# Moving the gating and most of the expert choice of a mixture-of-experts layer into the tail of the attention before it

## What is computed

```python
scores = jax.nn.sigmoid(x @ gate_w)                       # x: layernormed rows, 2048 x 512
group_scores = jnp.max(scores.reshape(T, 4, 8), axis=-1)
_, top_groups = jax.lax.top_k(group_scores, 2)            # scores outside them: -inf
_, selected_experts = jax.lax.top_k(masked_scores, 6)
weights = take_along_axis(scores, selected_experts); weights = weights / sum(weights)
# rows sorted by expert, then for each expert
d = (silu(xs @ w_gate[e]) * (xs @ w_up[e])) @ w_down[e]
expert_out = sum over the six of d * weight
shared = silu(x @ sw_gate) * (x @ sw_up) @ sw_down
return expert_out + shared
```

## Time and profile before

| | us |
|---|---|
| median of 3 runs | 2407.72 (2406.47 to 2412.87) |
| profiled execution | 2406.69 |
| its span, first to last instruction | 2404.6 |
| TensorE busy | 1983.8 (83%) |
| VectorE busy | 1051.7 (44%) |
| GpSimd busy | 1149.9 (48%) |
| ACT busy | 542.0 (23%) |
| mean granted clock of TensorE | 0.911 |

### The profile page before, as it was taken

The page is one execution under the profiler, slowest core; times in us unless marked ns, Lnnn a source line. Parts: engine busy times, 40 slices in busy tenths (PEclk is TensorE's granted clock), DMA queues, the critical chain, the costliest instruction groups (busy, mean ns, idle before and its releaser), DMA issues. The chain is left out here.

```text
span 2404.6 us, 33128 instructions
## 1 busy us (share of the span) xinstructions
PE 1983.8 (83%) x10463; PEld 1425.6 (59%) x10464; DVE 1051.7 (44%) x2035; ACT 542.0 (23%) x1148; POOL 1149.9 (48%) x578
## 2 busy tenths in 40 slices
PE   6947887968854889998699969999999999999910
PEld 3414443423322334332499959999999999999810
DVE  2564442067673567673575323333333333333300
ACT  3221221101102445442212212222221222222100
POOL 0000000003552465553615667667666878781886
PEclk8977997979985889999799989999999999999965
DMA  3051004121114344451304445545545555553999
GB/s 111 0 150 57 18 27 174 45 80 53 70 70 153 116 153 159 151 174 58 111 25 181 161 144 164 167 156 162 159 163 163 175 163 184 172 163 90 207 156 195
DMA packets 199484, 305.23 MB, mean 127 GB/s; under 512 B 16472, under 2 KB 94808, under 8 KB 199416
## 3 DMA queue, kind: packets, MB, share of 16 engines
q1 hardware_dynamic: 141624, 186.98, 24.5%
q0 software_dynamic: 21504, 50.74, 9.3%
q10 hardware_dynamic: 36288, 66.59, 8.0%
HBM read 186.16 MB, written 118.10 MB: 127 GB/s over the span
## 5 line engine op out<-in xcount | busy, mean ns | idle before, releaser
L2091 PE MATMUL psum<-e_gu_high,e_rowT_high 128*128 (+1 forms) x1272 | 428.7, 338 | 1.8 <-issue 1.6
L2091 PE MATMUL psum<-e_gu_low,e_rowT_high 128*128 (+1 forms) x1272 | 411.0, 325 | 0.0
L1744 ACT ACTIVATE e_silu<-psum 128x352 f32<-128x352 f32 x159 | 74.0, 466 | 867.0 <-PE psum L2096 844.9
L2096 PE MATMUL psum<-e_gu_high,e_rowT_low 128*128 (+1 forms) x1272 | 257.3, 324 | 11.3 <-DVE e_rowT_low L1812 11.3
L2091 PEld LDWEIGHTS psum<-e_gu_high,e_rowT_high 128*128 128x128 f32 x1272 | 240.4, 189 | 24.1 <-issue 18.8
L2091 PEld LDWEIGHTS psum<-e_gu_low,e_rowT_high 128*128 128x128 f32 x1272 | 241.4, 190 | 4.1
L2096 PEld LDWEIGHTS psum<-e_gu_high,e_rowT_low 128*128 128x128 f32 x1272 | 214.5, 189 | 11.6 <-DVE e_rowT_low L1812 11.6
L1821 DVE TENSOR_TENSOR e_midT_low<-psum,e_midT_high 128x256 fp32r<-128x256 f32 x159 | 67.4, 424 | 312.8 <-ACT e_midT_high L1753 310.5
L2111 PE MATMUL psum<-e_d_high,e_midT_high 128*128 (+3 forms) x477 | 188.8, 396 | 1.0 <-ACT e_midT_high L1753 1.0
L1717 POOL DMA_INDIRECT X<-d_y,f_slots x96 | 148.1, 1543 | 83.9 <-DVE e_y L1841 53.3
L2111 PE MATMUL psum<-e_d_low,e_midT_high 128*128 (+3 forms) x477 | 188.0, 394 | 0.0
(11 more groups left out here) (338 smaller groups left out, 3669.7 us busy)
## 6 DMA issues: line engine op xcount, KB each, us to landing
d_sorted<-y_zeros SPq DMA_DIRECT2D x32, 1040.0 KB, 8.6
d_y<-e_y ACTq DMA_DIRECT2D x127, 256.0 KB
e_row<-d_sorted ACTq DMA_DIRECT2D x125, 260.0 KB
e_gu_in<-in_L_ffn_w_gate SPq DMA_DIRECT2D x32, 704.0 KB, 4.4
e_gu_in<-in_L_ffn_w_up SPq DMA_DIRECT2D x32, 704.0 KB, 5.0
e_d_in<-in_L_ffn_w_down SPq DMA_DIRECT2D x32, 512.0 KB
d_y<-y_zeros SPq DMA_DIRECT2D x8, 1024.0 KB, 5.6
e_d_in<-in_L_ffn_w_down SPq DMA_DIRECT2D x32, 192.0 KB
```

Of the source, the lines that this page charges most:

```text
L2091: nc.tensor.matmul(bank[:, 0:M].unsqueeze(1), rowT_high[par][:, k, :], w[:, bass.ds(buffer, 1), k, at:at + M], start=(k == 0 and n == 0), ...
L2096: last = nc.tensor.matmul(bank[:, 0:M].unsqueeze(1), rowT_low[par][:, k, :], gu_high[:, bass.ds(buffer, 1), k, at:at + M], start=False, st ...
```

## The change

- `hold_routing` keeps `hs`, set 0's input tiles, the gate weights, the small constants and an arena of SBUF through both stages; tiles of the attention are laid over them (for instance `prob` for even groups over the arena, the q and k rows over set 0's input), and so the waits on what lies below change.
- In the attention VectorE makes the spread of a batch (`row_spread`) in groups 9 and 13, GpSimd its power, VectorE the normed rows (`norm_row`) of batch 0 in groups 10 and 11 and of batch 1 in groups 14 and 15, each behind the group's last `find_max`. The zero stores are spread over 12 groups.
- The loop ends at group 15; what followed is written out by hand. TensorE turns and gates batches 0 and 1, then 2, between the sums and values of the last group; projects tiles 12 to 15 in two alternating banks; then turns and gates batch 3. The choice for tiles 0 to 11 (class `Choice`) runs on VectorE between the last `add_out`s, up to `mark_hot` and `add_members`.
- SP loads set 0 at the end of the attention. In the new stage the split of set 0 is shared: ACT and VectorE make the gate part's high and low, GpSimd the rest; then GpSimd splits set 1.
- VectorE makes the whole choice for tiles 12 to 15 ahead of `shared_steps(0)`, marks and counts before `shared_steps(1)`. `COUNTED` goes from 7 to 2, `PLACED` from 9 to 4, `find_slots(0)` comes after tile 3, the last after tile 5.
- A row carries all six weights and all six expert numbers (524 floats). The column copies and their waits are gone. A routed tile picks its weight with `scalar_tensor_tensor`: columns whose expert number equals the tile's expert, times weights, summed in the accumulator.

```diff
-            for g in range(GROUPS + 6):
-                if 1 <= g <= GROUPS:
+            for g in range(GROUPS):
+                if g >= 1:
                     invert_sums(g - 1)
...
+                if g in (9, 13):
+                    row_spread(g // 4 - 2)
+                if g in (10, 11, 14, 15):
+                    t = g // 4 * JT - 2 * JT + g % 2 * 2
+                    norm_row(t)
+                    norm_row(t + 1)
+            add_out(11)
+            row_spread(2)
+            invert_sums(GROUPS - 1)
+            for t in range(2 * JT, 3 * JT):
+                norm_row(t)
+            scale_values(GROUPS - 1, 0)
+            scale_values(GROUPS - 1, 1)
+            dve.wait_ge(choice_loaded, 5 * 16)
+            dve.wait_ge(exped, 1)
+            first.invert()
+            add_out(12)
+            first.rank_groups()
+            add_out(13)
+            first.find_top()
+            add_out(14)
+            first.find_index()
+            add_out(15)
+            row_spread(3)
+            first.weigh().then_inc(weighed, 1)
+            for t in range(3 * JT, NT):
+                norm_row(t)
+            first.mark_hot()
+            first.add_members()
...
+            pe.wait_ge(added, 11)
+            project(11)
+            pe.wait_ge(exp_ready, ALL_EXP)
+            pe.wait_ge(choice_loaded, 5 * 16)
+            turn_batch(0)
+            sum_prob(GROUPS - 1)
+            turn_batch(1)
+            main_values(GROUPS - 1, (0, 1, 2, 3))
+            pe.wait_ge(max_ready, ALL_MAX)
+            gate((0, 1))
+            last_values(GROUPS - 1)
+            turn_batch(2)
+            gate((2,))
+            turn_logits(1, 3 * E_)
+            pe.wait_ge(added, 12)
+            project(12)
+            pe.wait_ge(last_scaled, GROUPS)
+            project(13)
+            pe.wait_ge(added, 13)
+            project(14)
+            pe.wait_ge(added, 14)
+            project(15)
+            turn_batch(3)
+            gate((3,))
+            turn_logits(2, P)
...
-            pool.wait_ge(rows_ready, B)
-            split(0, 0, 0)
+            nc.gpsimd.tensor_tensor(gu_high[:, 0, :, M:2 * M], gu_in[:, :, M:2 * M], ones[:, 0:1].unsqueeze(2).broadcast_to((P, CC, M)), ALU.mult).then_inc(high_ready, 1)
+            pool.wait_ge(high_ready, 1)
+            nc.gpsimd.tensor_tensor(gu_low[:, 0, :, M:2 * M], gu_in[:, :, M:2 * M],
+                                    gu_high[:, 0, :, M:2 * M].bitcast(F32), ALU.subtract).then_inc(up_split, 1)
+            split_down(0, 2)
             split(1, 1, 1)
...
-                nc.vector.tensor_copy(row_weight[par][:], row[par][:, D:D + 1]).then_inc(weight_taken, 1)
+                nc.vector.scalar_tensor_tensor(picked[par][:], row[par][:, D + TOPK:ROW], expert, row[par][:, D:D + TOPK],
+                                               ALU.is_equal, ALU.mult, accum_out=row_weight[par][:]).then_inc(weight_taken, 1)
...
+            dve.wait_ge(set_high, 1)
+            nc.vector.tensor_tensor(gu_low[:, 0, :, 0:M], gu_in[:, :, 0:M], gu_high[:, 0, :, 0:M].bitcast(F32),
+                                    ALU.subtract).then_inc(gate_split, 1)
             low_rowT(0, 0)
-            invert_scores()
+            last_batch.invert()
+            last_batch.rank_groups()
+            last_batch.find_top()
+            last_batch.find_index()
+            last_batch.weigh().then_inc(weights_ready, 1)
             shared_steps(0)
-            rank_groups()
+            last_batch.mark_hot()
+            last_batch.add_members()
+            add_before()
             shared_steps(1)
-            find_top()
             shared_steps(2)
-            find_index()
+            lay_out_tiles()
             shared_steps(3)
...
+            place_rows()
+            find_slots(0)
+            shared_steps(4)
```

More of the change, by code:

```diff
@@ L1 @@
+import math
 from contextlib import ExitStack
@@ L1088, in _, with hold_routing, area @@
                     last.then_inc(kv_done, 1)
+E_ = 32
+TOPK = 6
+EG = 4
+EPG = E_ // EG
+M = 352
+SLOT_TILES = TOK * TOPK // P + E_
+ROUTED_TILES = SLOT_TILES - 1
+SHARED_TILES = 2 * NT
+TILES = SHARED_TILES + ROUTED_TILES
+ROW = D + 2 * TOPK
+SCATTERS = 2
+GATHERS = 4
+def hold_routing(nc, c, stack):
+    c.hs = sbuf(nc, stack, "f_hs", [P, NT, ROW])
+    c.mv = sbuf(nc, stack, "f_mv", [P, NT, 2])
+    c.rstd = sbuf(nc, stack, "f_rstd", [P, NT])
+    c.index = sbuf(nc, stack, "f_index", [P, NT, 8], U32)
+    c.gu_in = sbuf(nc, stack, "f_gu_in", [P, CC, 2 * M])
+    c.d_in = sbuf(nc, stack, "f_d_in", [P, 3, D])
+    c.w_gate = sbuf(nc, stack, "f_w_gate", [P, CC, E_])
+    c.iota = sbuf(nc, stack, "f_iota", [P, E_])
+    c.part = sbuf(nc, stack, "f_part", [P, 1])
+    c.earlier = sbuf(nc, stack, "f_earlier", [P, EG, EG])
+    c.steps_of = sbuf(nc, stack, "f_steps", [P, NT])
+    c.arena = sbuf(nc, stack, "f_arena", [P, 16 * S])
+    at = 0
+    def area(*shape):
+        nonlocal at
+        n = math.prod(shape)
+        held = c.arena[:, at:at + n]
+        at += n
+        letters = "abc"[:len(shape)]
+        if len(shape) == 1:
+            return held
+        return held.rearrange(f"p ({' '.join(letters)}) -> p {' '.join(letters)}", **dict(zip(letters, shape)))
+    c.score = area(NT, E_)
+    c.hot = c.arena[:, at:at + TOPK * NT * E_].rearrange("p (k t e) -> p k t e", k=TOPK, t=NT)
+    c.hot_flat = c.arena[:, at:at + TOPK * NT * E_]
+    at += TOPK * NT * E_
+    c.member = area(NT, E_)
+    c.members_before = area(NT, E_)
+    c.best = area(NT, EG)
+    c.pair = area(NT, EG * EG).rearrange("p t (a b) -> p t a b", a=EG)
+    c.pair2 = area(NT, EG * EG).rearrange("p t (a b) -> p t a b", a=EG)
+    c.top = area(NT, 8)
+    c.indexf = area(NT, 8)
+    c.wsum = area(NT)
+    c.logitsT = area(S)
+    c.rowsT = area(CC, S)
@@ L1171, in _ @@
                     load_rows(g + 2)
[L1172 removed]
+                for n in range(blanks * g // 12, blanks * (g + 1) // 12) if g < 12 else ():
                     sp.dma_start(blank[n], zeros[:].unsqueeze(1).broadcast_to((P, JT, ROW))).then_inc(zeros_stored, 16)
@@ L1729, in _ @@
         def _(act):
-            def copy_rowsT(b):
-                for k in range(CC):
-                    act.wait_ge(rows_turned, b * CC + k + 1)
-                    if b >= 2 and k == 0:
-                        act.wait_ge(gated, 1)
-                    nc.scalar.copy(rowsT[b % 2][k], c.bank[k]).then_inc(rowsT_ready, 1)
             def load(i, par):
@@ L1898, in find_top @@
-            def find_top():
-                kept = best[:].unsqueeze(3).broadcast_to(by_group)
-                link(nc.vector.tensor_tensor(grouped(score), grouped(score), kept, ALU.mult))
-                link(nc.vector.tensor_scalar(best[:], best[:], -1.0, None, ALU.add))
-                link(nc.vector.tensor_tensor(grouped(score), grouped(score), kept, ALU.add))
-                for t in range(NT):
-                    last = nc.vector.max(top[:, t, :], score[:, t, :])
-                link(last)
@@ L1907, in find_index @@
-            def find_index():
-                for t in range(NT):
-                    last = nc.vector.max_index(index[:, t, :], top[:, t, :], score[:, t, :])
-                link(last)
-            def weigh():
-                link(nc.vector.tensor_copy(indexf[:], index[:]))
-                link(nc.vector.reduce_sum(wsum[:], top[:, :, 0:TOPK], AX.X))
-                link(nc.vector.reciprocal(wsum[:], wsum[:]))
-                nc.vector.tensor_tensor(weights[:], top[:, :, 0:TOPK], wsum[:].unsqueeze(2).broadcast_to((P, NT, TOPK)),
-                                        ALU.mult).then_inc(weights_ready, 1)
@@ L1919, in mark_hot @@
-            def mark_hot(first, end):
-                for k in range(first, end):
-                    last = nc.vector.tensor_tensor(hot[:, k], iota[:].unsqueeze(1).broadcast_to(wide),
-                                                   indexf[:, :, k:k + 1].broadcast_to(wide), ALU.is_equal)
-                link(last)
-            def add_members(first, end):
-                for k in range(first, end):
-                    if k == 1:
-                        link(nc.vector.tensor_tensor(member[:], hot[:, 0], hot[:, 1], ALU.add))
-                    else:
-                        link(nc.vector.tensor_tensor(member[:], member[:], hot[:, k], ALU.add))
+            last_batch = Choice(nc, chain, c, NT - JT, NT)
```

477 lines of the change are left out of this document (252 added, 225 removed).

## The result

| | before | after |
|---|---|---|
| median, us | 2407.77 (2406.05 to 2412.87) | 2393.14 (2387.45 to 2397.61) |
| ratio | 1 | 0.9939, 95% interval 0.9927 to 0.9951 |
| profiled execution, us | 2406.69, span 2404.6 | 2395.94, span 2394.2 |

What follows compares the result with a forecast made beforehand. TensorE's expert tiles and final gathers bound the kernel, so only an earlier first routed tile pays: 1421.2 - 1415 + 1.6 = 7.8 us sooner, 2400 us by the median, range 2379 to 2412.

Steps and rivals of the forecast that it cites:

- my own mechanism: At the routed stage's start VectorE is held until GpSimd's splitting ends: 2395 to 2407 us, chance 0.6.
- The scatters: Beside the shared tiles: 96 scatters start at 1236, take 155 to 164 us, end before those tiles; 21.9 us wait goes.
- The hold: Last batch's choice on VectorE waits beside GpSimd's splitting of sets 0 and 1; low part of tile 1 at 1205.
- S: Time at which the routed stage's first GpSimd instruction starts, forecast at 1169 us.
- one grant in five: Beside streaming GpSimd, VectorE gets in at one instruction boundary in five: two or three instructions at some 12 boundaries.
- The stage's start: End of the attention, last batch's transposes and gate partly at half clock: routed stage starts at 1169, bounds 1165 to 1173.
- The loop's own loss: Attention groups 9 to 15: nine more VectorE pieces delay the loop by 1.2 us, at most some 5.
- From A on: From tile 1's low part, forecast at 1205: 208.6 us plus 1 of waiting, TensorE at the first routed tile at 1415.
- what lies behind the first routed tile: Routed tiles and final gathers: all alike, except 1.6 us saved because the slow restart after the pause goes.
- VectorE would hardly be held: Routed stage's start: low part of tile 1 comes 12 us after it, TensorE 29 us sooner, 2379 us; chance 0.2.
- The collision in the loop: Attention groups 10, 11 and 14: norms collide with GpSimd's additions, 21 us lost, 2421 us; chance 0.11.
- The scatters didn't end last: Denies the rival that scatters, 15 us later than forecast, still end last before the routed tiles: 2404 to 2412 us; chance 0.09.

Runs made afterwards that it cites:

- e4: The changed kernel with counting after shared tile 8 instead of 2 and placing after 10 instead of 4, so the scatters start later: 2424.4 us, ratio 1.0086.
- e2: The changed kernel with GpSimd splitting set 1 only after the last batch's weights are done: 2392.08 us, ratio 0.9951.
- e10: The changed kernel with score, group sums and second pair table of the last batch's choice in PSUM, weights, marking and counting later: 2374.55 us, ratio 0.9858.
- e3: The changed kernel with set 1 split by ACT before tile 9 and VectorE before tile 10 instead of by GpSimd: 2376.37 us, ratio 0.9885.
- e1: The changed kernel run again, unaltered, as the measure for the other runs: 2394.25 us, ratio 0.9946.

## Why the prediction held, point by point

The forecast was 2400.0, the measured median 2393.14, inside the range and on the side that had most of the chance. It is 1.9 us below the 2395 to 2407 that I gave my own mechanism, and the gain is 14.6 us by the medians where I had 7.8. The profiled pair is 10.7 us apart, 3 more than forecast, most of it a term that I left out (below). The other 3.9 us are the scatter of executions: the profiled one before is 1.1 us below its median, the one after 2.8 above. Its main steps against the profile after:

**The scatters: right.** First at 1235.4 (forecast 1236), 163.7 us long (155 to 164), no wait for `e_row`; e4 shows that this is what the change earns. The slack was smaller than the 15 us I gave: the row loads were issued at 1403.6, and with e4's 2.8 us behind that the rows were there some 8.5 us before 1414.93.

**The hold: right in size, half wrong in its working.** Low part of tile 1: S+34.7, forecast S+36 within S+12 to S+39. I had spread one grant in five evenly over the boundaries. In fact VectorE got in at each of the five boundaries from 1175.7 to 1185.5, inside set 0, and at none of the next five, so that one instruction alone took up 14.22 us. That S+34.7 is so near S+36 is in part luck: 14.22 of the 34.7 us are one addition's, and e2 shows other instructions let in at each of four such boundaries. And I had left it open whether a `tensor_tensor` with two SBUF inputs is held, as L968 in the earlier trace rows ran free beside a power. It is, by L1174, L1175 and e2's marking; e10 shows the second SBUF operand to be the reason. L968 was the wrong neighbour: that a power of 64 columns and 12.5 us hardly reads, where the splitting streams, is my reading of the difference, and no run tests it. Beside the splitting all this fits the Trainium skill (SBUF — State Buffer, Who interferes with whom): two SBUF inputs contend, so do a `tensor_scalar` and a cast from SBUF to SBUF, a reduction (L1170, 0.29 us) doesn't. Beside the power it doesn't fit, as L968 ran its 2.31 us a piece unhindered, and there the measurement decides. By the rule I had put the choice at S+37, the better reason though not the better number.

**The stage's start: 1172.84 against 1169, in the bounds.** Five terms, 4.0 us together. The transposes and the gate at the half clock took 3.67 and 6.06 us, where I had 3.4 and, with one slow product, 4.5: 1.9 us. In group 14 of the attention TensorE's granted clock fell to half, which no reading of before could show; the stretches (columns as above), and the same ones of e3:

```profile
1088.00:1090.00 2.00, 2.00 (x17) 1.09 (x10) 1.71 (x3) 0.57 (x1) 2.00 (x1) 0.50 0.67 164
1090.00:1092.00 2.00, 2.00 (x3) 0.96 (x4) 1.19 (x2) 1.37 (x2) 2.00 (x2) 0.50 1.04 372
1092.00:1094.00 2.00, 2.00 (x3) 0.67 (x2) 0.00 (x0) 0.00 (x0) 1.83 (x2) 0.51 0.79 292
```
```profile
1088.00:1090.00 2.00, 2.00 (x6) 0.85 (x5) 0.63 (x1) 0.33 (x1) 2.00 (x2) 1.00 1.03 366
1090.00:1092.00 2.00, 2.00 (x13) 0.57 (x15) 1.00 (x2) 0.00 (x0) 1.74 (x2) 1.00 0.84 311
```

That group took 23.78 us instead of the 21.24 of e2: 2.5 us. Only the profiles after, of e1 and of e4 have it, not the nine other runs of the same loop; why stays open. The loop's own loss by the nine new pieces is 0.5 us (two groups of 21.57 and 21.50 instead of 21.3), less than the 1.2 I took. The loop had started 1.2 us later than before (900.88 against 899.67), which is run-to-run, and the four projections gave back 0.9 (13.93 instead of four times 3.70).

**From A on.** From the low part of tile 1 to the first routed row 207.4 us, forecast 209.6. These 2.2 us and the hold's 1.3 gave back 3.5 of the start's 3.8, which is why the arrival, 1414.93 against 1415, looks better than the working was.

**The mis-sized term: what lies behind the first routed tile.** I said all is alike there but for the restart (1.6, measured 1.8). It is 2.05 us shorter still, and 1.3 to 2 us shorter in the other runs without a wait for `e_row` and without a standstill (790.5 to 791.2 us). That term, missing, is most of the distance between the forecast and the profiled pair: 2406.7 - 7.8 is 2399, and 2395.9 was measured; the rest is 0.3 us in the gathers and 0.6 elsewhere. The cause wasn't tried. It is not `take_weight`, which got dearer than my 0.2 us. From the groups by line of before, the copy of the weight (busy us, mean 141 ns), and from the tile view after, what stands in its place:

```profile
L1817 DVE COPY e_row_weight<-e_row 128x1 f32<-128x1 f32 x127 | 17.9, 141 | 0.0
```
```profile
L2040 DVE SCALAR_TENSOR_TENSOR e_picked<-e_row,f_arena x127: 211/215/2391, 1416.9 to 2272.4; 128x6 f32<-128x6 f32 x127
```

Six columns, two of its operands in SBUF: 215 ns at the median, up to 2391, 821 on average. The 65 that came up while GpSimd split nothing took 213 ns on average, the 62 beside its splitting 1458, and these end with the GpSimd instruction that they met. So it is held like the choice was, and costs nothing only because VectorE had the idle time of the earlier trace rows.

**The rivals.** That VectorE would hardly be held is what e10 makes true, 2374.55 us; I had 2379 for it. The collision in the loop didn't come: GpSimd was idle when the norms ran (the first two at 1009.98 to 1010.98, GpSimd idle until 1016.99). The scatters didn't end last.

## What to carry to other kernels

Before putting VectorE work beside streaming GpSimd work, look where each operand lies: with at most one in SBUF it runs at its own price, with two (or SBUF to SBUF in a cast or `tensor_scalar`) one instruction of 0.2 us stood for 14 here. Moving GpSimd's work behind it only passes the hold on; take it off GpSimd, or move an operand to PSUM. When a wait is removed, read what is ahead of it on the same path: here 21.9 us were removed, and 10.7 of them were lost at once to a longer wait for VectorE's choice, which the same change had put in one piece beside the splitting.

## What the runs showed that I had not expected

With three or four indirect scatters of 262 KB under way instead of two, the scatters took 122 us instead of 166, and the kernel became 106 us slower: TensorE, VectorE and ACT stood still for whole stretches of 20 us, TensorE with nothing in the profile to wait for. The waits for landing that look like waste, 60 of 165 us, go with the only setting in which the other engines ran.

One and the same instruction is let in at the same boundary each time (14.22 or 14.23 us in four runs), but which boundary that is follows no pattern that I found: L1175 was passed by five times beside set 1, the marking of e2 was let in at six boundaries running there, and the picks of the routed tiles at the first that they met.
